# Attention sums of a graph network kept in two PSUM banks at register addresses, copied out by ScalarE

## The reference

```python
q, k, v = x @ Wq + bq, x @ Wk + bk, x @ Wv + bv          # (6250, 8, 32) each
scores = einsum('ehd,ehd->eh', q[src], k[dst]) / sqrt(32)
m = segment_max(scores, dst)
e = exp(scores - m[dst]);  z = segment_sum(e, dst)
out = segment_sum(v[src] * (e / z[dst])[:, :, None], dst)
```

## Time and profile before

| | |
|---|---|
| median of three runs | 3706.06 us (3704.23 to 3707.38) |
| span of the profiled execution | 4137.2 us |
| the attention loop in it, 765 to 2151 us | 1386 us, 110 turns |
| DVE / PE / ACT busy in the loop | 1125 / 1011 / 653 us |
| granted TensorE clock in the loop | 0.89 |

### The profile page before, as it was taken

How to read it: one execution, slowest core, us unless ns; L and a number is a source line. 1 busy time by engine, 2 the same in 40 slices (tenths; PEclk the granted TensorE clock), 3 DMA queues, 4 the chain that set the end, 5 groups by cost and what they waited for, 6 DMA issues and landing times. The chain is left out here.

```text
span 4137.2 us, 55464 instructions
## 1 busy us (share of the span) xinstructions
PE 3002.7 (73%) x12662; PEld 2413.6 (58%) x12662; DVE 3401.4 (82%) x9121; ACT 2194.8 (53%) x5961; POOL 1969.1 (48%) x2404
## 2 busy tenths in 40 slices
PE   3545444577777777677756688988988888888866
PEld 2434333455555555555545567777777777777754
DVE  8999996687888888788878378888888888888877
ACT  3235542444444444444438466666665666666557
POOL 1000003556666666666620366666666666666400
PEclk9867777788998889888988899999999999999988
DMA  2111004666667666666636655655655666556361
GB/s 65 39 55 38 13 26 148 191 202 208 202 208 216 207 209 208 211 205 209 206 98 174 172 161 168 173 163 168 171 168 167 167 172 170 166 167 170 89 145 50
DMA packets 295230, 635.60 MB, mean 154 GB/s; under 512 B 78197, under 2 KB 147123, under 8 KB 294657
## 3 DMA queue, kind: packets, MB, share of 16 engines
q0 software_dynamic: 141312, 463.96, 38.3%
q1 hardware_dynamic: 153602, 168.11, 14.5%
HBM read 587.26 MB, written 44.65 MB: 153 GB/s over the span
## 5 line engine op out<-in xcount | busy, mean ns | idle before, releaser
L2469 POOL DMA_INDIRECT area<-d_xr,col x880 | 890.2, 1012 | 686.8 <-DVE area L2706 236.8
L2562 PE MATMUL ms_near_a<-low,ms_hotT 128*128 x1760 | 550.4, 395 | 204.3 <-issue 99.2
L2066 PE MATMUL at_out<-at_pv,at_hot 128*128 128x264 f32 x1760 | 558.6, 447 | 75.7 <-issue 32.0
L2020 POOL DMA_INDIRECT low<-d_qv,col x440 | 449.6, 1022 | 265.6 <-DVE at_pv L2196 129.1
L2563 PE MATMUL ms_near_c<-tab_c,ms_hotT 128*128 x1760 | 536.1, 387 | 0.0
L2046 PE MATMUL at_kx<-area,tab_c 128*128 x1760 | 508.8, 417 | 21.8 <-issue 20.7
L2562 PEld LDWEIGHTS ms_near_a<-low,ms_hotT 128*128 128x128 f32 x1760 | 327.6, 192 | 301.6 <-issue 258.9
L2066 PEld LDWEIGHTS at_out<-at_pv,at_hot 128*128 128x128 f32 x1760 | 358.9, 217 | 161.9 <-issue 63.1
L2046 PEld LDWEIGHTS at_kx<-area,tab_c 128*128 128x128 f32 x1760 | 372.9, 213 | 96.0 <-issue 25.3
L2238 DVE SCALAR_TENSOR_TENSOR area<-area,tab_c,at_out 128x264 f32 x440 | 211.7, 481 | 216.4 <-remote 114.9
L2604 ACT COPY area<-area 128x2 f32<-128x2 f32 x440 | 82.0, 186 | 566.0 <-DVE area L2675 379.0
(11 more groups left out here) (375 smaller groups left out, 6560.6 us busy)
## 6 DMA issues: line engine op xcount, KB each, us to landing
tab_c<-by_dst_marks SPq DMA_DIRECT2D x110, 512.0 KB
ms_near_no<-by_src_near SPq DMA_DIRECT2D x110, 224.0 KB
area<-d_xr,col POOLq DMA_INDIRECT x880
d_qv<-low SPq DMA_DIRECT2D x10, 1120.0 KB, 5.0
low<-d_qv,col POOLq DMA_INDIRECT x448
d_xr<-mid_hm SPq DMA_DIRECT2D x5, 1128.8 KB, 6.8
first_x<-in_x_dram SPq DMA_DIRECT2D x5, 1120.0 KB
tab_c<-in_x_dram SPq DMA_DIRECT2D x5, 1120.0 KB, 7.0
```

What stands on the lines that cost most here:

```text
L2020: pool.indirect_dma_start(out=ring[t.n % SLOTS][:, k, :], out_offset=None, in_=m.d_qv, in_offset=bass.IndirectOffsetOnAxis(ap=col[:, t.h, ...
L2066: last = TE.matmul(out[:, p % 2, 0:AW], hot[:, t.h % 2, j, :], pv[:, t.h % 2, j].rearrange("p h d -> p (h d)"), start=(k == 0), stop=(k == ...
L2469: pool.indirect_dma_start(out=far_rows(t, p)[:, k, :], out_offset=None, in_=m.d_xr, in_offset=bass.IndirectOffsetOnAxis(ap=col[:, t.h, SPA ...
L2562: TE.matmul(near_a[:, (SPAN * p + k) % 4, 0:TW], rows, m.tab_a[:, bass.ds(at, TW)], start=True, stop=True)
```

## The change

The sums of a block are no longer taken out after each step. A block's steps add up in one PSUM bank, the next block's in the other (odd and even blocks), for as long as the window lasts.

- DVE: the 440 additions (`add`) are gone. `rescale` now multiplies by `keep` and `fac` in one instruction, once a window, and waits for ACT's copies (`kept`). Before the second turn a new function works out, in 13 small instructions on one partition, the tables of addresses (`pe_spots`, `act_spots`). Two memsets are new.
- PE: at a window's first step an identity matmul puts the rescaled row from SBUF back into the bank (line 2060 of the changed kernel). At each of the 7 other steps two matmuls of zeros, 2 columns each, in bf16, open one bank and close the other (lines 2064, 2065). PE reads 12 more addresses a turn into registers (two more loads), and it waits for ACT's copy of the step before (`kept`).
- ACT: at each step it copies a bank (128 x 264) into `m.acc_l0` (line 2174): at a window's first step the running bank, else the other bank, whether or not a block has ended. Its work of a turn is cut into pieces, with one copy between each.

```diff
+                def go_on(t, p):
+                    if not t.exists():
+                        return
+                    w, j = step_of(t, p)
+                    if p == 0:
+                        if t.n == 0:
+                            pe.wait_ge(spotted, 1)
+                        spots.fetch(t.n * 2 * SG, 2 * SG)
+                        others.fetch(t.n * 2 * SG, SG)
+                    if j == 0:
+                        pe.wait_ge(rescaled, w + 1)
+                        bank, old = spots.values(p, 1, OUT_TOP)[0], spots.values(SG + p, 1)[0]
+                        TE.matmul(out[:, bass.ds(bank, AW)], m.ident[:, :], m.acc_l0[:, bass.ds(old, AW)], start=True, stop=False)
+                        return
+                    begin, close = (out[:, CLEAR:][:, bass.ds(at, 2)] for at in (spots.values(SG + p, 1, OUT_TOP)[0], others.values(p, 1)[0]))
+                    pe.wait_ge(kept, w * STEPS + j - 1)
+                    TE.matmul(begin, zeros[:, :], zeros[:, 0:2], start=True, stop=False)
+                    TE.matmul(close, zeros[:, :], zeros[:, 0:2], start=False, stop=True).then_inc(opened, 1)
...
-                    if p >= 2:
-                        pe.wait_ge(summed, t.n * SG + p - 1)
-                    elif t.plus(-1).exists():
-                        pe.wait_ge(summed, t.plus(-1).n * SG + p + 3)
+                    go_on(t, p)
+                    at = spots.values(p, 1, OUT_TOP)[0]
+                    ends = step_of(t, p)[1] == STEPS - 1
                     for k in range(SPAN):
                         j = SPAN * p + k
-                        last = TE.matmul(out[:, p % 2, 0:AW], hot[:, t.h % 2, j, :], pv[:, t.h % 2, j].rearrange("p h d -> p (h d)"),
-                                         start=(k == 0), stop=(k == SPAN - 1))
+                        last = TE.matmul(out[:, bass.ds(at, AW)], hot[:, t.h % 2, j, :], pv[:, t.h % 2, j].rearrange("p h d -> p (h d)"),
+                                         start=False, stop=(ends and k == SPAN - 1))
...
+                def keep_block(t, p):
+                    if not t.exists():
+                        return
+                    w, j = step_of(t, p)
+                    if p == 0:
+                        if t.n == 0:
+                            act.wait_ge(spotted, 1)
+                        spots.fetch(t.n * 2 * SG, 2 * SG)
+                    if j == 0:
+                        if w == 0:
+                            return
+                        act.wait_ge(out_in, w * STEPS)
+                    else:
+                        act.wait_ge(opened, w * (STEPS - 1) + j)
+                    if w or j > 1:
+                        act.wait_ge(kept, w * STEPS + j - 1)
+                    A.copy(m.acc_l0[:, bass.ds(spots.values(SG + p, 1, (NB - 1) * AW)[0], AW)],
+                           out[:, bass.ds(spots.values(p, 1)[0], AW)]).then_inc(kept, 1)
...
                 def period(t):
+                    ready, old = t.plus(-LAG), t.plus(-LAG - 1)
+                    keep_block(old, 0)
+                    far_columns(t.plus(1))
                     hot_columns(t.plus(1))
+                    keep_block(old, 1)
+                    hot_rows(ready, 0)
                     w = window_before(t)
                     if w:
                         weights(w)
-                    hot_rows(t.plus(-LAG))
-                    weight_sums(t.plus(-LAG))
-
+                    keep_block(old, 2)
+                    hot_rows(ready, 1)
+                    weight_sums(ready)
+                    keep_block(old, 3)
...
+                def work_out_spots():
+                    ln = Links(dve, spot)
...
+                    ln.mark(V.tensor_copy(odd, blk[0:1, 1:1 + SUPER]))
+                    ln.mark(V.tensor_tensor(same, blk[0:1, 1:1 + SUPER], blk[0:1, 0:SUPER], ALU.is_equal))
+                    ln.wait()
+                    ln.mark(V.tensor_single_scalar(odd, odd, 1, ALU.bitwise_and))
+                    ln.wait()
+                    ln.mark(V.tensor_scalar(bank, odd, 512.0, None, ALU.mult))
+                    ln.mark(V.tensor_scalar(other, odd, -512.0, 512.0, ALU.mult, ALU.add))
+                    ln.mark(V.tensor_tensor(begin, odd, same, ALU.not_equal))
...
+                    dve.sem_inc(spotted, 1)
...
-                def rescale(t, at):
+                def rescale(t):
+                    starts.fetch(t.n * SG, 1)
                     dve.wait_ge(fac_in, t.window + 1)
...
-                    V.tensor_tensor(block_at, block_at, bcast(fac[:, :], HD), ALU.mult).then_inc(rescaled, 1)
-                    dve.wait_ge(rescaled, t.window + 1)
+                    if t.window:
+                        dve.wait_ge(kept, t.window * STEPS)
+                    block = m.acc_l0[:, bass.ds(starts.values(0, 1)[0], AW)].rearrange("p (h d) -> p h d", d=HD)
+                    V.scalar_tensor_tensor(block, block, keep[:, t.window:t.window + 1], bcast(fac[:, :], HD), ALU.mult, ALU.mult).then_inc(rescaled, 1)
...
-                def add(t, p, at):
-                    if not t.exists():
-                        return
-                    dve.wait_ge(out_in, t.n * SG + p + 1)
-                    row = m.acc_l0[:, bass.ds(at[p], AW)]
-                    if p or t.plus(-1).exists():
-                        dve.wait_ge(summed, t.n * SG + p)
-                    V.scalar_tensor_tensor(row, row, keep[:, bass.ds(t.n * SG + p, 1)], out[:, p % 2, 0:AW], ALU.mult, ALU.add).then_inc(summed, 1)
```

More of the change, by code:

```diff
@@ L1819, in fetch, with values @@
         self.eng.load(self.regs[0:n], self.off[0:1, bass.ds(at, n)])
-    def values(self, first, n):
-        return [self.eng.snap(r, min_val=0, max_val=self.top) for r in self.regs[first:first + n]]
+    def values(self, first, n, top=None):
+        return [self.eng.snap(r, min_val=0, max_val=self.top if top is None else top) for r in self.regs[first:first + n]]
     def load(self, at, n):
@@ L2180, in _ @@
                 V.memset(m.area.rearrange("p (b a) -> p b a", a=AW)[:, :, DIM:AW], 0.0).then_inc(made, 1)
+                V.memset(zeros[:, :], 0.0).then_inc(made, 1)
+                V.memset(out, 0.0).then_inc(made, 1)
                 dve.wait_ge(c_in, 32)
[L2182 to L2184 removed]
+                first_steps = lambda at: blk[:, at:at + SUPER].rearrange("p (w j) -> p w j", j=STEPS)[:, :, 0]
@@ L2185, in _ @@
+                V.tensor_tensor(keep, first_steps(1), first_steps(0), ALU.is_equal).then_inc(made, 1)
+                dve.wait_ge(made, 9)
+                starts = Starts(dve, "at_dve", off, (NB - 1) * AW, 1)
                 HEAD0, TAIL0 = 0, WSTEPS + 2
+                def work_out_spots():
+                    ln = Links(dve, spot)
+                    rows = pv.rearrange("p t k h d -> p (t k h d)")[0:1]
+                    bank, other, begin, same = (rows[:, n * SUPER:(n + 1) * SUPER] for n in range(4))
+                    odd = rows[:, 4 * SUPER:5 * SUPER].bitcast(I32)
+                    part = lambda ap, v: ap.rearrange("o (g v j) -> o g v j", v=2, j=SG)[:, :, v, :]
+                    steps = lambda ap: ap.rearrange("o (g j) -> o g j", j=SG)
+                    ln.mark(V.tensor_copy(odd, blk[0:1, 1:1 + SUPER]))
[6 more added lines that the diff above has]
+                    ln.mark(V.tensor_tensor(begin, odd, same, ALU.not_equal))
+                    ln.mark(V.tensor_scalar(part(act_spots, 1), steps(off[0:1, :]), float(-AW), 0.0, ALU.add, ALU.max))
+                    ln.wait()
+                    ln.mark(V.tensor_copy(part(pe_spots, 0), steps(bank)))
+                    ln.mark(V.tensor_scalar(part(pe_spots, 1), steps(begin), 512.0, None, ALU.mult))
+                    ln.mark(V.tensor_copy(part(act_spots, 0), steps(other)))
+                    ln.wait()
+                    ln.mark(V.tensor_copy(part(pe_spots, 1)[:, ::WG, 0], steps(off[0:1, :])[:, ::WG, 0]))
+                    ln.mark(V.tensor_copy(part(act_spots, 0)[:, WG::WG, 0], steps(bank)[:, WG - 1:AGROUPS - 1:WG, SG - 1]))
+                    ln.mark(V.tensor_copy(part(act_spots, 1)[:, WG::WG, 0], steps(off[0:1, :])[:, WG - 1:AGROUPS - 1:WG, SG - 1]))
+                    ln.wait()
+                    dve.sem_inc(spotted, 1)
```

58 lines of the change are left out of this document (34 added, 24 removed).

## The result

The changed kernel takes 3850.9 us (3847.96 to 3852.41, four runs) and the kernel before 3705.1 (3701.55 to 3707.38). The ratio is 1.040, with a 95% interval of 1.038 to 1.041: 146 us slower. The prediction said 3629 us, and its range ended at 3765.

What follows compares the result with a forecast made beforehand. No engine alone was the bound, as DVE and PE wait in turn; PE becomes fullest. Loop 1386 + 189 new PE work - 275 idle = 1300 us, 86 less, times 0.896 gives 77; 3706 - 77 = 3629 us, range 3525 to 3765.

Steps and rivals of the forecast that it cites:

- 220 in all, at 0.52 us each: PE's two added register loads a turn, ahead of its first matmul: 0.55 us a turn exposed, 60 us (20 to 120).
- of its 375 us of idle time some 275 should go: PE's idle time in the loop: waits for DVE's maxima shrink once the additions queued ahead of them are gone.
- the hundred that would stay: PE idle time left in the loop, 100 us, since a window's maxima still go four times between the engines.
- My factor of 0.896: Median run of 3706 us against the profiled span, 431 us longer; scales the loop's gain, assuming the loop shrinks like the rest.
- my 1300: Forecast loop time in us: PE's work of 1200 plus 100 idle, 86 less than the profiled 1386.
- 916 to 950: DVE's work in the loop, in us, after the 440 additions go, down from 1125 busy.
- POOL's floor: POOL's gathers in the loop: 854 us busy plus 249 us between gathers, 1103 us that no cheaper DVE shortens.
- I had 0.375: ACT's 440 copies out of PSUM, 0.375 us each, 165 us, costed at nothing as hidden in ACT's idle stretches.
- I had 0.20 and 77: PE's 385 pairs of zero matmuls: 0.20 us a pair, 77 us in all, between 62 and 150.
- where I had 0.44: PE's identity matmul at each of 55 window starts: 0.44 us each, 24 us in all.
- PE's sequencer is the path: Rival: loads and register waits stop PE queuing matmuls ahead; loop grows by 101 us, 3796 us; chance 0.16.
- The clock falls: Rival: small gaps between PE's groups at each step lower the mean clock to 0.80; 3750 us; chance 0.06.

Runs made afterwards that it cites:

- second profile of the kernel before: The unchanged kernel before, profiled again when it ran in about 3704 us, since the first profile's span was 4137 us; it took 3705.99 us, span 3704.2.
- loads in twos: Changed kernel with its address table reordered and read two values at a time, on PE behind the previous step's columns, on ACT ahead of each copy: 3710.3 us, 1.001.
- the kernel before with live loads: Kernel before plus PE loads of 8 and 4 zeros ahead of a turn's first sums, added to the sums' address: 3949.9 us, 1.067; at a long time 4174.5, 1.007.

## Why the prediction was wrong

- **The step that failed first: "220 in all, at 0.52 us each".** I took the duration of a load of two values for loads of eight and four. They take 1.92 and 0.99 us, 320 us on the sequencer in place of 114, and 239 us of it with the array standing still in place of my 60 (20 to 120). The mechanism, loads ahead of a turn's first matmul with only the `near` step to cover them, was the one that I had written down. Its size was four times mine, and twice my upper end. Loads of 2.91 us a turn go far beyond the cover of 0.86 us, where my 1.04 us hardly did.
- **The step that failed second: "of its 375 us of idle time some 275 should go".** Those were waits of the profiled execution. In the second profile of the kernel before PE idles 218 us, so 275 were never there to be had, and DVE waits 22 us for the sums. Of the 218, all but the 38 us that PE idles outside the loads did go, 180 us. The 275 were also not worked out: I set the hundred that would stay. My factor of 0.896 shrank the loop to 1242 us, where it is 1165: it was not evenly stretched, and the second layer less so. The loop of the changed kernel, 1311 us, is by chance close to my 1300.
- **DVE.** Its busy time fell by 151 us in the loop, to 966; I had 916 to 950. But it gave nothing back: first PE's loads set the pace, and without them POOL's floor. I had that floor at 1103 us, and it is 1123. I set it 197 us under PE's 1300, but the kernel before already ran on it and on DVE together, and without the loads the changed kernel stops on it (3710 us).
- **ACT.** Copies take 0.377 us (I had 0.375). In the change with loads in twos all of them stand and the time is the old one, so there they cost nothing over POOL's floor; that all of them are hidden is not shown, as the copy at a window's start stands ahead of the rescale.
- **PE's other terms.** By the medians of both profiles a step's columns are followed by its sums after 0.92 us, where it was 0.86, and the sums by the next columns after 0.97, where it was 0.89: 0.13 us for the pair and its register work, 51 us in all. I had 0.20 and 77. The Trainium skill, TensorE: Matmul & The Clock Gate, section "Back-to-back issue gap", has 81 ns for a weight load and a matmul of 128 moving columns, from which I had estimated 0.16. The matmuls here move 2 columns, so this is no trace of that figure, and 0.13 lies below the estimate. The identity matmul takes 0.54 us (1509.04 to 1509.58, and 0.54 in the median) where I had 0.44, 30 us in place of 24. With both in place the kernel with twos loses nothing.
- **The sum again.** Measured against the second profile the loop is 1165 + 30 + 51 + 239 - 180 = 1305 us, and it took 1311; the 6 us left are within what the clock, 0.93 before and 0.92 after, can add. Mine was 1386 + 189 - 275 = 1300. So of the 232 us between my -86 and the measured +146, 179 are the loads and 95 the idle time, and the smaller terms take 42 off.
- **The rivals.** "PE's sequencer is the path" was right in kind, at 3796 us with a chance of 0.16; fully exposed loads were priced there at 121 us. "The clock falls", with 0.06, is a small second part of the loss: from before to after the clock goes from 0.94 to 0.92 in the stretch; between 12 values a turn at one place and 8 it is worth 0.74 us a turn. But the cause was not the one that I had named, small gaps at each step: the twos have a pair of zeros at each step too, and their clock is 0.95. By the Trainium skill, TensorE: Matmul & The Clock Gate, section "A second HAM failure mode: psum-queue depth-cycling", the cycling through banks should lower the clock. The page has it of one bf16 kernel of 512 columns, and every kernel here cycles through two banks, the one before too, so no run here tests it.

**What would have shown it.** The trace of before held a load of four values on DVE, 0.95 us, beside PE's 0.52 for two:

```profile
L1819 DVEq TENSOR_LOAD <-at_off x110: 942/946/1174, 763.3 to 2144.6; - x110
```

With that, as an estimate of 0.24 us a value, the loads would have been 2.9 us a turn against at most 0.86 us of cover: 2.0 us a turn exposed, 225 us, and the forecast slower.

## What to carry to other kernels

Count the values of a register load, not only the loads, and look at what the array has queued when the load starts: loads of two, 8 values a turn spread behind the columns of each step, were free, and 12 values at one place cost 141 us more than these, and 247 in the kernel before. With two of eight gathers gone, 8 values at one place cost only 7 us more than in twos, so the first thing to try is to load fewer values. Before summing what an engine gives back, add up the other engines with the gaps between their instructions; an engine whose gaps are all 0.3 us and wait for nobody is full, even at a busy share of 75%. And when the span of the profile is 12% over the runs, profile again and take no wait from it as a quantity that can be given back.

## What the runs showed of the hardware

- A load of values into registers costs about 0.24 us a value on PE (0.52, 0.99 and 1.92 us for 2, 4 and 8), 1.72 us for 8 on ACT and 0.47 for 2, and on DVE 0.29 for one and 0.95 for four.
- In the changed kernel the load of eight starts 0.02 us (median) after the last queued weight load starts, and the array then finishes what it holds, 0.7 us, and stands still. In the kernel before with live loads it starts 1.05 us after it, and the array stands still for 1.67 of the 1.92 us.
- The granted clock falls to 1.2 GHz behind the stops. Of the falls between 760 and 1840 us, all 46 of the changed kernel and 62 of 63 of the kernel before with live loads come within 3.0 us after the end of a load of eight. The mean is 0.92 and 0.90 in these two, with 2.9 us of loads a turn at one place, and 0.98 with 1.9 us. Kernels without such loads, in the profiles taken when the kernel before ran in some 3704 us, lie between, 0.94 to 0.97, so the mean does not follow the length of the stop alone.
- An indirect gather on POOL takes 1.03 us and is followed by the next after 0.3 us when nothing holds it up: eight of them are 10.6 us a turn.
